# Two of eight quantisation groups rounded through a 32-bit integer on ScalarE, with ScalarE's own scaling in place of VectorE's

## What is computed

```
# stage 0: quantise in groups, 8 thresholds / deltas / zero points
gi  = sum(|x| <= thresholds);  d, zp = deltas[idx], zero_points[idx]
y   = (clip(round(x / d) + zp, 0, 63) - zp) * d,  0 where gi == 8
x   = x + y
# stage 1: adapter weight chosen per batch element
x   = x + x @ weight[adapter_ids].T
# stage 2: shared weight and a low-rank part
x   = x + x @ W.T + 0.5 * (x @ lora_A[labeler]) @ lora_B_w.T
# stage 3: low-rank adapter
x   = x + (x @ B[adapter_ids]^T) @ A[adapter_ids]^T
```

## Time and profile before

| | |
|---|---|
| median of 3 runs | 483.93 us (483.61 to 484.32) |
| span of the profiled execution | 481.9 us |
| what lies around the span (median less span) | 2.0 us |
| TensorE busy | 464.9 us, 96% |
| VectorE busy | 419.4 us, 87% |
| ScalarE busy | 358.6 us, 74% |
| TensorE's granted clock over the span | 0.996 |

### The profile page before, as it was taken

The page is one execution under the profiler, slowest core; times in us unless marked ns, Lnnn a source line. Parts: engine busy times, 40 slices in busy tenths (PEclk is TensorE's granted clock), DMA queues, the critical chain, the costliest instruction groups (busy, mean ns, idle before and its releaser), DMA issues.

```text
span 481.9 us, 8215 instructions
## 1 busy us (share of the span) xinstructions
PE 464.9 (96%) x3184; PEld 424.7 (88%) x3184; DVE 419.4 (87%) x481; ACT 358.6 (74%) x383; POOL 45.5 (9%) x46
## 2 busy tenths in 40 slices
PE   3999869999999999999999999999999999999997
PEld 3969669898999989898999989898999989898995
DVE  5999999999999899989999899989999899989120
ACT  6979958678877879678877879678887879675011
POOL 1064000200002000200002000210003000100000
PEclk9999989999999999999999999999999999999999
DMA  7997214712335122712335122712335122702002
GB/s 282 407 415 258 113 34 149 294 54 97 131 127 212 44 95 97 294 44 103 131 120 218 44 89 101 294 44 103 131 101 237 44 86 104 294 2 88 1 1 87
DMA packets 17830, 67.07 MB, mean 139 GB/s; under 512 B 2576, under 2 KB 5904, under 8 KB 13712
## 3 DMA queue, kind: packets, MB, share of 16 engines
q1 hardware_dynamic: 17808, 66.81, 37.9%
HBM read 56.84 MB, written 9.96 MB: 139 GB/s over the span
## 4 chain that ended last, share of the span: by engine, by line
PE 90%; ACT 3%; DMA 3%; DVE 2%; issue 1%; POOL 1%; SPq 0%; DVEq 0%
PE x_bank L603 45%; PE acc L628 34%; PE acc L579 3%; PE x_bank L616 3%; PE acc L640 2%; PE acc L638 2%; DMA w1b<-w 2%; DMA rows<-own_rows 1%; ACT mask L344 1%; ACT w2h L400 1%; DVE y L460 1%; PE acc L567 1%; ACT tq L329 1%; PE acc L577 0%; ACT outb L404 0%
## 5 line engine op out<-in xcount | busy, mean ns | idle before, releaser
L603 PEld LDWEIGHTS x_bank<-x,w1b 128*128 128x128 f32 x2048 | 233.2, 193 | 8.2 <-issue 4.9
L603 PE MATMUL x_bank<-x,w1b 128*128 128x128 f32 x2048 | 234.8, 276 | 3.7 <-DVE x L475 3.7
L344 ACT ACTIVATE mask<-absx,negtop 128x1024 bf16<-128x1024 f32 x112 | 128.4, 1146 | 40.3 <-DVE y L460 39.5
L329 ACT ACTIVATE tq<-xin,magic,rdelta 128x1024 f32<-128x1024 f32 x128 | 157.0, 1234 | 0.6 <-DVE yhigh L526 0.3
L460 DVE COPY_PREDICATED y<-mask,uq 128x1024 f32<-128x1024 int16 x112 | 151.1, 1349 | 0.1
L439 DVE TENSOR_SCALAR tq<-tq,par 128x1024 f32<-128x1024 f32 x128 | 99.2, 775 | 3.7 <-DVE y L460 3.1
L448 DVE TENSOR_SCALAR uq<-tq,ylow,yhigh 128x1024 f32<-128x1024 f32 x112 | 92.3, 824 | 0.2 <-DVE y L460 0.2
L628 PE MATMUL acc<-w2h,x2h 128*128 128x512 f32 x256 | 80.9, 393 | 2.0 <-DVE x2l L481 2.0
L628 PE MATMUL acc<-w2h,x2l 128*128 128x512 f32 x256 | 79.9, 390 | 0.0
L628 PE MATMUL acc<-w2l,x2h 128*128 128x512 f32 x256 | 79.2, 390 | 0.0
L295 POOL TENSOR_TENSOR w1b<-w1b,eye 128x256 f32<-128x256 f32 x32 | 36.5, 1140 | 368.9 <-DMA w1b<-w 368.9
(11 more groups left out here) (57 smaller groups left out, 218.9 us busy)
## 6 DMA issues: line engine op xcount, KB each, us to landing
w1b<-w SPq DMA_DIRECT2D x32, 1024.0 KB, 6.7
xin<-x SPq DMA_DIRECT2D x16, 512.0 KB, 3.7
out<-outb SPq DMA_DIRECT2D x14, 512.0 KB, 2.8
w1b<-w2n SPq DMA_DIRECT2D x4, 1024.0 KB, 10.6
ring<-w2t SPq DMA_DIRECT2D x6, 512.0 KB, 6.7
ua<-e_dram SPq DMA_DIRECT2D x16, 128.0 KB, 2.5
ua<-w2t SPq DMA_DIRECT2D x2, 512.0 KB, 7.8
va<-la SPq DMA_DIRECT2D x8, 128.0 KB, 2.7
```

The source lines that it names most:

```text
L329: nc.scalar.activation(tq[:, n % TQ, :], flat(xin, c % UN), ACT.Identity, bias=magic[:, 0:1], scale=rdelta[:, g:g + 1]).then_inc(t_ready, 1)
L344: nc.scalar.activation(mask[:, n % MK, :], absx[:, :], ACT.Relu, bias=negtop[:, g:g + 1], scale=1.0).then_inc(mask_ready, 1)
L603: last = nc.tensor.matmul(x2_bank[2 * t + i][:, o % HALF * P:(o % HALF + 1) * P], w1b[:, o, at:at + P], x1[:, t, k, :], start=(o % HALF == ...
```

## The change

From step n = 16 on (the third unit), the steps with n mod 8 = 2 and n mod 8 = 5 go another way. On ScalarE `multiple(n)` becomes two instructions: x / delta is written as a 32-bit integer into the `tq` buffer (the conversion rounds), and behind a wait for that, the integer is read, multiplied by delta and written back as float32. VectorE's `value(n)` is left out for these steps, and `clamp(n)` waits for ScalarE's second instruction instead. There are 14 units with two such steps each, so 28 `value` go and 28 ScalarE instructions are added. The semaphores' counts follow. Masks, buffers, selection and all other steps stay.

```diff
--- before.py
+++ after.py
@@ -13,6 +13,7 @@
 
 
     f32, f32r, bf16, i16 = mybir.dt.float32, mybir.dt.float32r, mybir.dt.bfloat16, mybir.dt.int16
+    i32 = mybir.dt.int32
     ALU = mybir.AluOpType
     ACT = mybir.ActivationFunctionType
 
@@ -127,6 +128,8 @@
         t_ready = sem("t_ready")
         mask_ready = sem("mask_ready")
         u_ready = sem("u_ready")
+        level_ready = sem("level_ready")
+        act_value = sem("act_value")
         clamped = sem("clamped")
         y_ready = sem("y_ready")
         y_cut = sem("y_cut")
@@ -159,6 +162,17 @@
 
         def group_of(n):
             return G - 1 - n % G
+
+        INT_FROM, INT_AT = PER, (2, 5)
+
+        def on_levels(n):
+            return n >= INT_FROM and n % G in INT_AT
+
+        def act_values(n):
+            return sum(on_levels(i) for i in range(n + 1))
+
+        def dve_values(n):
+            return n + 1 - act_values(n)
 
         def selections(n):
 
@@ -326,6 +340,14 @@
                     act.wait_ge(x_in[c % UN], 16 * (c // UN + 1))
                 if n >= TQ:
                     act.wait_ge(clamped, n - TQ + 1)
+                if on_levels(n):
+                    slot = tq[:, n % TQ, :]
+                    nc.scalar.activation(slot.bitcast(i32), flat(xin, c % UN), ACT.Copy,
+                                         scale=rdelta[:, g:g + 1]).then_inc(level_ready, 1)
+                    act.wait_ge(level_ready, act_values(n))
+                    nc.scalar.activation(slot, slot.bitcast(i32), ACT.Copy, scale=par[:, 1, g:g + 1]) \
+                        .then_inc(act_value, 1)
+                    return
                 nc.scalar.activation(tq[:, n % TQ, :], flat(xin, c % UN), ACT.Identity, bias=magic[:, 0:1],
                                      scale=rdelta[:, g:g + 1]).then_inc(t_ready, 1)
 
@@ -435,13 +457,18 @@
         def _(dve):
             def value(n):
                 g = group_of(n)
-                dve.wait_ge(t_ready, n + 1)
+                if on_levels(n):
+                    return
+                dve.wait_ge(t_ready, dve_values(n))
                 nc.vector.tensor_scalar(tq[:, n % TQ, :], tq[:, n % TQ, :], -MAGIC, par[:, 1, g:g + 1],
                                         ALU.add, ALU.mult).then_inc(u_ready, 1)
 
             def clamp(n):
                 g = group_of(n)
-                dve.wait_ge(u_ready, n + 1)
+                if on_levels(n):
+                    dve.wait_ge(act_value, act_values(n))
+                else:
+                    dve.wait_ge(u_ready, dve_values(n))
                 if n % G == 1 and n >= G:
                     dve.wait_ge(x1_ready, n // G)
                 clamped_y = uq[:, n % 2, :] if n % G else y[:, :]
```

## The result

The changed kernel takes 488.65 us (median of 19 runs, 486.34 to 489.84), the kernel before 484.79 us in as many runs beside it (483.61 to 487.54). The ratio is 1.0051, with a 95% interval of 1.0031 to 1.0072. So the change makes the kernel slower, by about 0.5%. The direction is the forecast's, 485.2 us with a range up to 487.2; the size is not, and the median lies above the range.

What follows compares the result with a forecast made beforehand. TensorE, busy 96% of the span, sets the end, with VectorE nearly as loaded and delivering x1. Span 481.9 + 1.4 - 0.1 = 483.2 us, with 2.0 around it 485.2; range 483.3 to 487.2.

Steps and rivals of the forecast that it cites:

- The shift of the bank: ScalarE's first rounded bank before a batch's unit t = 0, and x1 behind it, come 0.55 us later.
- The wait at t = 0: TensorE's weight load at the start of unit t = 0 waits 0.39 us for x1 in the mean.
- the slack: At t = 0, x1 may come some 0.3 us later before a batch lengthens: 0.16 mean slack plus 0.15 absorbed.
- VectorE's saving: Removed `value`, 1.3 us per unit, stand ahead of VectorE's wait for ScalarE's rounded bank: worth nothing to x1.
- the waits at t = 1: Six TensorE waits for x1 at starts of unit t = 1, 0.37 us each, costing 0.22, were to stay.
- the sum over the batches: Batches 2 to 7 each lose 0.39 - 0.15 = 0.24 us at the start of t = 0, 1.4 us in all.
- move together: GpSimd's work stretches VectorE's L468 from 1.29 to 1.62 us; left unchanged, though coming apart could be worth 0.3 per batch.
- Batch 1: Its stretch still carries work on the tables; removed `value` may bring x1 forward, taken as 0.1 us gained.
- Hidden: Rival: larger slack at t = 0 or a cheap pair means no change, 483.9 us; chance 0.29.
- Faster: Rival: VectorE's 1.3 us saving per unit reaches x1, the six t = 1 waits go, 482.5 us; chance 0.09.
- Integers are slow: Rival: ScalarE's new instructions take twice as long, shift about 2.6 us, 498 or more; chance 0.06 shared with growing contention.
- Contention that grows: Rival: contention between engines grows, some 0.15 us per batch in the range's upper end; chance 0.06 shared with slow integers.

Runs made afterwards that it cites:

- e5: Kernel before with two ScalarE copies of 440 columns into a spare tile at steps n mod 16 = 5; 485.58 us lower group, ratio 1.0053.
- e6: Kernel before with four such ScalarE copies into a spare tile at steps n mod 16 = 5; 492.97 us lower group, ratio 1.0184.
- e1: Changed kernel with the pair only at n mod 16 = 2, 10 and 13, VectorE scaling at 5 as before; 483.97 us lower group, ratio 0.9979.
- e3: Kernel before without VectorE's scaling at the change's steps, nothing put in its place; 484.15 us lower group, ratio 1.0016.
- e8: Changed kernel with twelve tiny VectorE memsets at VectorE's start; 485.51 us lower group, ratio 1.0036.
- e10: Kernel before with twelve tiny VectorE memsets at VectorE's start; 484.09 us lower group, ratio 0.9983.
- e7: Kernel before with one ScalarE copy of 440 columns into a spare tile at steps n mod 16 = 5; 483.81 us lower group, ratio 1.0008.
- e4: Changed kernel with the pair at n mod 8 = 1 from n = 17 on, in place of 2 and 5; 481.77 us lower group, ratio 0.9970.
- e9: Changed kernel with the pair at n mod 8 = 1 from n = 9 on, in place of 2 and 5; 482.02 us lower group, ratio 0.9959.
- e2: Changed kernel with the pair at n mod 16 = 5 alone, all else as before; 485.82 us lower group, ratio 1.0033.

## Why the prediction was right and wrong

**The mechanism was right, term by term.** The pair was put at 2.24 us and measured 2.22. The shift of the bank, 0.55, was 0.52. The wait at t = 0, 0.39, was 0.41. The loss per batch, 0.24, was 54.61 - 54.36 = 0.25 in the first batch period, which has no other disturbance. That it fits so closely is in part luck: the shift came out 0.03 smaller, and so did the slack, at 0.52 - 0.25 = 0.27 (0.20 to 0.24 by e5 and e6) in place of 0.31. The slack of 0.16 was counted with 0.05 us from x1 to a waiting load, which is the row of t = 1; at t = 0 a waiting load starts 0.12 to 0.13 behind x1 (261.72 against 261.60), so that part was nearer 0.1. Three of the four pairs are covered (e1). VectorE's saving in the steady part is worth nothing (e3), and the waits at t = 1 stayed. By itself the mechanism gives what e8 shows over its control e10, +1.4 us, where the forecast had +1.3; over before it is +1.7.

**The step that failed is the sum over the batches.** "Batches 2 to 7 do, six times 0.24 = 1.4 us" took one batch for all. The six periods of the profiled execution lost 0.25, 0.55, 0.58, 0.34, 0.70 and 0.25 us, 2.67 in all, and 2.7 is also what the lower group lost. Two gaps of VectorE of 0.36 us over the usual one are 0.7 us of the difference; they fall on `value` at n mod 8 = 1, between split and x1, where nothing is left to take them up, and they go away when VectorE's program is shifted (e8). The trace of before had no such gap to be read. Another 0.3 is the `clamp` at 204.44, longer beside GpSimd's work, which has nothing like it in e8: the prediction had said that GpSimd's and VectorE's work "move together" and left the term at nothing, with 0.3 us per batch if they came apart. They came apart in one batch. Some 0.2 us are left without a cause.

**The range failed by the two groups of runs.** It was built on three runs of before that all fell into the earlier group, and took 2.0 us around the span as fixed. The median of 488.65 is one of the later group. In the earlier one, the time is 486.57, inside the range, though still 1.4 us above the forecast.

**Batch 1 was mis-sized, and differently in the two groups.** "I take 0.1 us as gained." In the earlier group e1's batch 1 starts at 95.97, before at 96.26: 0.3. In the later group TensorE waits for x1 at the start of batch 1, and VectorE's saving does reach it. e7 has all of VectorE's scaling, e3 doesn't:

```profile
99.75 1.41 PEld L611 LDWEIGHTS x_bank<-x,w1b 128*128 128x128 f32 x12 [1.90 <-issue]
```

```profile
98.62 0.97 PEld L626 LDWEIGHTS x_bank<-x,w1b 128*128 128x128 f32 x8 [0.93 <-issue]
```

1.0 us less of a wait. Each of these is one profile. It fits that the changed kernel's later group is only 1.8 us over before's (488.95 against 487.19), and e3's under it (486.34 against 487.01). So the rival "VectorE's saving reaches x1" looks right for one batch of eight, in some of the runs.

**The rivals.** *Hidden* needed a slack of more than 0.52; it is 0.20 to 0.27. *Faster* named the right condition, a removed instruction that VectorE isn't waiting around: e4 puts it there and is faster by 2.1 us. *Integers are slow* falls with L345 and L348 (its shift would be about 2.8 us by the prediction's own rows and not 2.6; nothing rests on it). *Contention that grows* is right for the one `clamp`.

**What stays open.** Why the head of an execution has two lengths. In the profiles of the later group TensorE starts unit 1 at 68.8 to 69.0 us (e4 68.1, e9 67.3) in place of 65.5 to 66.0, and in e7's head it waited 3.8 us for the second split bank of unit 0 where before waited 2.0. The two part early: in five of the six later ones (e2, e3, e4, e7, e8) SyncE issues the first piece of `w1b` behind its wait at 18.0 to 18.7 us in place of 16.9 to 17.5, and GpSimd begins its add on the fourth at 37.6 to 38.6 in place of 36.8 to 37.4; e9 doesn't follow this. What sets it off isn't shown. Nor is what the gaps of VectorE are.

## What to carry to other kernels

Where two engines hand over in a chain, look at each removed or added instruction with the wait behind it: ahead of a wait for someone else its saving is nothing; behind it, what the chain delivers comes sooner (x1 by 0.73 us in e4), and the receiver gains what it had lost by waiting (0.2 us a batch), whatever the engine's share of busy time. Pairs of the same two instructions cost 2.7 us at one set of steps and gained 2.1 at another. Where every repeat of a loop has a slack of a few tenths of a microsecond, one repeat doesn't stand for all: once a change has used the slack up, a small irregularity has nothing to take it up. So measure several repeats, and several executions, before a sum is made.

## What the runs showed of the hardware

- VectorE has, at a few places of its program, a gap of 0.55 to 0.57 us where the same step otherwise has 0.20, with an instruction that waits for VectorE's own selection. The changed kernel and e3 have two of these, 80 instructions apart, and one of 0.48, at the same instructions; twelve tiny instructions at the start removed them (e8).
- A weight load on TensorE that waits 0.4 us for its data costs 0.2 to 0.25 us (the 0.37 of t = 1, for one, 54.36 - 54.17 = 0.19 a batch, which e4 gave back). A wait of 1.69 (e6) lengthened its half batch to 28.64 us against 26.99 in the kernel before, 1.65.
- What a GpSimd add costs the VectorE `clamp` (128 x 1024) that it overlaps depends on when it begins. Over batches 1 to 7 of the twelve profiles `clamp` takes 1.11 to 1.15 us where the add begins 0.14 us or more ahead of it, 1.28 to 1.38 where it begins from 0.01 ahead to 0.09 behind, and 0.81 to 0.82 where it begins 0.15 or more behind, as where no add is near.
- ScalarE's float32 to int32 and back takes 1.14 and 1.15 us for 128 x 1024, as the mask (1.15 us), which has one operand from a column of SBUF like them.
